# One chunk's square on ScalarE and TensorE instead of VectorE's product, in the edge scoring of a graph attention layer

## The reference

```
h_r   = einsum('nf,hfd->hnd', layernorm(x), W_r)       # 8 heads of 64 features
diff  = h_r[dst] - h_r[src]                            # per edge: 512 numbers
score = s_src + s_dst + sum(diff * a_dif) + sum(|diff| * a_abs) + sum(h_r[src] * h_r[dst] * a_prd)
alpha = leaky_relu(score, 0.2);  att = softmax of alpha over the edges of a source node
out   = sum over edges of att * h_e[dst]
```

## Time and profile before

| what | value |
|---|---|
| median of three runs | 1385.02 us |
| profiled execution | 1381.5 us, its span 1379.7 us |
| TensorE busy | 1239.5 us (90%), weight loads 803.8 us (58%) |
| VectorE busy | 1106.1 us (80%) |
| ScalarE busy | 736.3 us (53%) |
| GpSimd busy | 753.9 us (55%) |
| L794, products, 336 | 229.9 us busy, mean 684 ns |
| L790, subtractions, 204 and 132 | 138.7 and 89.9 us, mean 681 ns |
| L961, sums, 672 records | 91.6 us busy, mean 605 ns |
| L1003 and L1005, ScalarE, 336 each | 196.2 and 273.6 us, mean 584 and 814 ns |
| mean granted TensorE clock | 0.956 of full speed |

### The profile page before, as it was taken

One profiled execution on the slowest core, in us unless ns is written; L12 is line 12 of the kernel. 1 busy time (PEld: TensorE's weight loads), 2 busy tenths in 40 slices (PEclk: granted clock), 3 DMA queues, 4 the chain that ended last, 5 costly groups with the idle time before them and its releaser, 6 DMA issues. The chain is left out here.

```text
span 1379.7 us, 23782 instructions
## 1 busy us (share of the span) xinstructions
PE 1239.5 (90%) x6730; PEld 803.8 (58%) x6805; DVE 1106.1 (80%) x2258; ACT 736.3 (53%) x1237; POOL 753.9 (55%) x858
## 2 busy tenths in 40 slices
PE   6999986989999999999994999999999376999985
PEld 1555553545555555555552888877777244777762
DVE  8989897999999999999997998888888954122216
ACT  5555534888898989989993010000100653555541
POOL 1300016766666666666625777777777502566541
PEclk9999997999999999999996999999999776999998
DMA  9133338988888888888857798888887165343478
GB/s 249 70 122 147 123 124 299 310 290 273 281 300 285 304 294 280 296 285 302 279 167 182 241 318 289 292 296 283 290 268 242 48 228 181 131 134 131 136 256 328
DMA packets 141701, 322.60 MB, mean 234 GB/s; under 512 B 30163, under 2 KB 46279, under 8 KB 141595
## 3 DMA queue, kind: packets, MB, share of 16 engines
q0 software_dynamic: 62816, 212.87, 46.8%
q1 hardware_dynamic: 74524, 103.15, 22.1%
q10 hardware_dynamic: 4256, 5.24, 1.1%
HBM read 255.27 MB, written 65.93 MB: 233 GB/s over the span
## 5 line engine op out<-in xcount | busy, mean ns | idle before, releaser
L1309 PE MATMUL m_ps<-msg,hot 128*128 128x260 f32 x1344 | 304.9, 387 | 14.7 <-SPq L1106 14.7
L1309 PEld LDWEIGHTS m_ps<-msg,hot 128*128 128x128 f32 x1344 | 254.2, 191 | 65.5 <-issue 27.5
L1005 ACT ACTIVATE rows<-rows,raw_a 128x512 f32<-128x512 f32 x336 | 273.6, 814 | 11.2
L1146 POOL DMA_INDIRECT rows<-he_d,target x234 | 237.8, 1016 | 75.1 <-issue 65.5
L929 PE MATMUL gs_ps<-room,hot_t 128*128 x944 | 262.2, 383 | 10.6 <-DVE hot_t L783 3.8
L1227 DVE TENSOR_TENSOR msg<-rows,room 128x512 f32<-128x512 f32 x336 | 213.4, 690 | 40.3 <-DMA rows<-he_d,target 39.1
L794 DVE TENSOR_TENSOR rows<-rows 128x512 f32<-128x512 f32 x336 | 229.9, 684 | 3.1 <-ACT rows L1005 2.8
L1003 ACT ACTIVATE rows<-d_ps 128x512 f32<-128x512 f32 x336 | 196.2, 584 | 62.5 <-PE d_ps L942 61.3
L765 POOL DMA_INDIRECT x_sb<-table_d,target x150 | 148.1, 987 | 80.2 <-PE d_ps L942 48.1
L1163 ACT COPY room<-m_ps 128x520 f32<-128x520 f32 x20 | 11.8, 592 | 296.7 <-PE m_ps L1309 296.7
L929 PEld LDWEIGHTS gs_ps<-room,hot_t 128*128 128x128 bf16 x1008 | 92.0, 98 | 121.3 <-issue 79.1
(11 more groups left out here) (342 smaller groups left out, 1825.7 us busy)
## 6 DMA issues: line engine op xcount, KB each, us to landing
rows<-early_d SPq DMA_DIRECT2D x84, 256.0 KB, 4.3
early_d<-x_sb SPq DMA_DIRECT2D x51, 256.0 KB, 5.4
x_sb<-local_d SPq DMA_DIRECT2D x84, 128.0 KB, 5.1
early_d<-rows SPq DMA_DIRECT2D x33, 256.0 KB, 5.7
table_d<-rows POOLq DMA_DIRECT2D x10, 520.0 KB, 3.3
both_d<-rows POOLq DMA_DIRECT2D x10, 520.0 KB, 4.3
he_d<-he SPq DMA_DIRECT2D x20, 256.0 KB, 2.0
both_d<-he SPq DMA_DIRECT2D x20, 256.0 KB, 2.3
```

The costliest lines, as they stand in the source:

```text
L1005: act.activation(uv[:, j, c, :], ab[:, j, c, :], ACT.Identity, bias=raw[:, 0, c:c + 1], scale=raw[:, 1, c:c + 1]).then_inc(ur, 1)
L1146: pool.indirect_dma_start(g[:, r, t, :, :, :].rearrange("p c h d -> p (c h d)"), None, he_d, bass.IndirectOffsetOnAxis(ap=k["target"][:, q ...
L1309: last = pe.matmul(m_ps[:, bass.ds(slot[t], 1), j, 0:HEADS // 2 * HW].rearrange("p a f -> p (a f)"), hot[:, r, t, :], halves[:, r, t, j, : ...
```

## The change

A group with st below 12 has one squared chunk, c = 3 - st mod 4 (`squared`). For it ScalarE writes diff^2 to one of four buffers (`square`) and |diff| to `ab`, and leaves out w1 * |diff| + w0; VectorE leaves out the product. TensorE sums |diff| of that chunk with w0 as weights in place of ones, in the group's usual sum. Once in four groups, behind the transposes of t = 0, it sums the four squares with w1 as weights (`reduce_squares`). That is 3 rounds a strip, 18 in all. The weights lie in `head_w`, which VectorE fills at the start.

Three of the four square buffers lie in memory that other things used: in the scratch of the strip steps, and in the last strips of `al` and `fw`. The strip steps get their scratch elsewhere, and the third and fourth step of the fifth strip move behind those of the last.

```diff
+SQUARES = STRIPS // CH * CH
+def squared(n):
+    st = n % STRIPS
+    return CH - 1 - st % CH if st < SQUARES else None
...
-        first = home[:, 0:LC]
+        square = (s.sb("square0", [P, LC])[:, :], home[:, 0:LC], al[:, L - LC:L], fw[:, L - LC:L])
...
             def times(n, c):
-                dve.wait_ge(ur, CH * n + c + 1)
+                if c == squared(n):
+                    return
+                dve.wait_ge(ur, rank(n, c))
                 dve.tensor_tensor(uv[:, n % 2, c, :], uv[:, n % 2, c, :], ab[:, n % 2, c, :], ALU.mult).then_inc(vr, 1)
...
+                first = fw[:, hi:hi + LC] if tg < TG - 2 else square[TG - 1 - tg]
                 if step == 2:
                     link(dve.tensor_tensor(first, al[:, lo:hi], lead[:, lo:hi], ALU.add))
...
             link(dve.memset(extra[:, :, :, :, :, :], 0.0))
+            link(dve.memset(k["head_w"][:, :], 0.0))
+            spots = k["head_w"][:, 30:].rearrange("p (i c s) -> p i c s", i=2, c=CH)
+            mark(dve.tensor_copy(spots[0:D, :, :, 0], raw[0:D, :, :]))
+            link(dve.tensor_copy(spots[D:P, :, :, 1], raw[D:P, :, :]))
...
-                        strip_scores((n - 4 - step) // STRIPS - 1, step)
+                        tg = (n - 4 - step) // STRIPS - 1
+                        if tg < TG - 2 or step < 2:
+                            strip_scores(tg, step)
...
             for step in range(4):
                 strip_scores(TG - 1, step)
+            for step in range(2, 4):
+                strip_scores(TG - 2, step)
...
+                    if c == squared(n):
+                        last = pe.matmul(sc_ps[32 * c:32 * (c + 1), :], weight_of(0, c, st), ab[:, n % 2, c, :],
+                                         start=(st == 0), stop=final, tile_position=(0, 32 * c), skip_group_check=True)
...
+            def reduce_squares(n):
+                st = order[n][1]
+                pe.wait_ge(abr, CH * n + squared(n) + 1)
+                for c in range(CH):
+                    of = st - c
+                    last = pe.matmul(sc_ps[32 * c:32 * (c + 1), :], weight_of(1, c, of), square[c],
+                                     start=False, stop=False, tile_position=(0, 32 * c), skip_group_check=True)
+                last.then_inc(squares_red, 1)
...
                     if t == 2 and n >= 2:
                         reduce(n - 2)
+                    if t == 0 and n >= 2 and squared(n - 2) == 0:
+                        reduce_squares(n - 2)
...
+                if c == squared(n):
+                    if rounds(n) >= 1:
+                        act.wait_ge(squares_red, rounds(n))
+                    act.activation(square[c], d_ps[:, c % 2, :], ACT.Square)
                 act.activation(ab[:, j, c, :], d_ps[:, c % 2, :], ACT.Abs).then_inc(abr, 1)
+                if c == squared(n):
+                    return
```

More of the change, by code:

```diff
@@ L723, in score_edges @@
         kept = sem("strip_kept")
+        squares_red = sem("squares_reduced")
+        timed = lambda n: sum(squared(m) != c for m in range(n) for c in range(CH))
+        rank = lambda n, c: timed(n) + sum(squared(n) != d for d in range(c + 1))
+        rounds = lambda n: n // STRIPS * (SQUARES // CH) + n % STRIPS // CH
         early_out = [sem(f"early_out{j}") for j in range(RING)]
@@ L957, in reduce, with weight_of @@
                                   start=False, stop=False, skip_group_check=True)
+                if n == 0:
+                    pe.wait_ge(extras, 1)
+                if squared(n) is not None:
+                    pe.wait_ge(abr, CH * n + CH)
                 for c in range(CH):
                     if n == G - 1 or c == 0:
-                        pe.wait_ge(vr, CH * n + (c + 1 if n == G - 1 else CH))
-                    last = pe.matmul(sc_ps[32 * c:32 * (c + 1), :], heads[:, column], uv[:, n % 2, c, :],
-                                     start=(st == 0), stop=final, tile_position=(0, 32 * c), skip_group_check=True)
-                last.then_inc(red, 1)
+                        pe.wait_ge(vr, rank(n, c if n == G - 1 else CH - 1))
+                    if c == squared(n):
+                        last = pe.matmul(sc_ps[32 * c:32 * (c + 1), :], weight_of(0, c, st), ab[:, n % 2, c, :],
+                                         start=(st == 0), stop=final, tile_position=(0, 32 * c), skip_group_check=True)
+                    else:
+                        last = pe.matmul(sc_ps[32 * c:32 * (c + 1), :], heads[:, column], uv[:, n % 2, c, :],
+                                         start=(st == 0), stop=final, tile_position=(0, 32 * c), skip_group_check=True)
+                last.then_inc(red, 1)
+            def weight_of(i, c, st):
+                lo = 30 + (i * CH + c) * 32 - 2 * st
+                return k["head_w"][:, lo:lo + 32]
+            def reduce_squares(n):
[3 more added lines that the diff above has]
+                    of = st - c
+                    assert squared(n - c) == c
+                    last = pe.matmul(sc_ps[32 * c:32 * (c + 1), :], weight_of(1, c, of), square[c],
+                                     start=False, stop=False, tile_position=(0, 32 * c), skip_group_check=True)
+                last.then_inc(squares_red, 1)
             for n in range(G + 2):
@@ L1940, in kernel_body @@
                 k["not_before"] = flat[:, locals_at + F // 2:locals_at + F // 2 + Q]
+                k["head_w"] = flat[:, locals_at + F // 2 + Q:locals_at + F // 2 + Q + 30 + 2 * CH * 32]
                 k["turns"] = k["pick"].rearrange("p t c s h -> p (t c s h)").bitcast(U16)[0:1, 0:Q]
```

## The result

The changed kernel took 1389.91 us (median of five runs, 1386.90 to 1391.44) against 1385.33 of the kernel before: ratio 1.0042, 95% interval 1.0027 to 1.0056. It is slower, by 4.6 us at the medians; 1390.5 had been predicted.

The account below looks back on a forecast made before the run. TensorE was taken to bound the scoring stage at 5.69 us a plain group. VectorE -15.5, rounds +19.6 and moved steps +1.45 gave +5.5 us: 1390.5 us on the median of 1385.02, range 1384.5 to 1396.

Parts of the forecast that it names:

- TensorE is the pace: Scoring stage: a plain group is TensorE's own 5.69 us; VectorE is late only where something is added to it.
- Rival 1: Scoring stage: hand-overs, not TensorE, set the pace, so the change is faster by about 38 us, 1347 us; chance 0.06.
- the reading by the share of the weight loads: TensorE, plain stretch: weight loads busy only 16.16 of 28.44 us would make it little more than half full.
- A round costs 1.09 us, +19.6 in all: TensorE, scoring: 18 new rounds of four 32-column matmuls, each priced like a group's sum; ends +10.8 to +23.4.
- Rival 2: TensorE, scoring: a round costs only 0.5 to 0.8 us, its weights loading during other matmuls; slightly faster to even; chance 0.12.
- rival 3: Scoring: VectorE gives back 19 us and a round costs 0.99, so the change comes out even, 1385 us; chance 0.14.
- VectorE gives back 15.5 us: Scoring: 72 products fewer recover 11.0 us in the strips' four groups and 4.5 in the first 15 groups.
- The moved steps, +1.45: Stage end: two strip steps of the fifth strip move onto the serial path to the carry exchange, about +1.45 us.
- ScalarE is covered: Scoring: Square and Abs take about 1.2 us, ScalarE's group 5.2, below TensorE's 5.69; no cost, cover 0.5 us a group.
- Rival 4: Scoring: ScalarE becomes late, each 0.1 us beyond 5.7 a group costing 7 us; at 0.1, 1397.5 us; chance 0.06.
- The start is hidden: Before VectorE's first subtraction: a memset of 286 elements and two small copies fit in its 4.48 us idle time; no cost.
- the signs set for being wrong: Changed profile: groups without a round below 5.6 us, a round adding under 0.8 us, or TensorE waiting for ScalarE.

## Why the prediction was right

- *TensorE is the pace.* Right: a plain group stays at 5.7 us while VectorE's busy time in it falls from 27.79 of 28.44 us to 4.74 of 5.70, and taking the rounds out or doubling them moves the stage by 15.9 and 15.4 us. Rival 1, and with it the reading by the share of the weight loads, is excluded: the weight loads are busy 3.24 of 5.70 us (57%), and yet TensorE has no room for a round.
- *A round costs 1.09 us, +19.6 in all.* Right in a plain group (1.10), and for the reason given: the price was read from the same matmuls between the same neighbours, so it holds the 0.24 us of passing to 32 columns and back. The total is 15.9 when the rest stays as it is, since six of the 18 rounds fall beside a scan on VectorE. The prediction knew of that cover and entered it on the other side of the account, in VectorE's gain. Rival 2 is excluded (a round adds 1.10 us in a plain group, not 0.5 to 0.8), and so is rival 3 (VectorE gives back no 19 us). Rival 3's step from sum to next gather is 1.00 us in the earlier trace rows, not 0.99; its sum is 0.5 then, not 0.
- *VectorE gives back 15.5 us.* Counted as the prediction counts, with every round at its full 1.10, the second strip's four groups give 25.24 - 24.08 + 1.10 = 2.26 us and the others' 2.22 (predicted 2.2), and the first 15 groups 94.81 - 93.07 + 3.30 = 5.0 (predicted 4.5): 16.2 in all. As an effect of its own, without the rounds, it is 12.2. So neither term is what its engine does alone; the cover moves some 4 us between them and leaves the sum as it is. Sum of the two terms: +4.1 predicted, +3.7 measured.
- *The moved steps, +1.45.* Measured 1.44, on the serial path.
- *ScalarE is covered.* Right; Square runs 0.58 us, and Square to Abs is 0.48 from start to start (the prediction had about 0.6, so the engine's need was put a little high). Rival 4 is excluded for this kernel; at twice the Squares it begins.
- *The start is hidden.* The first sum came at 232.45 (before 233.18; 232.4 to 233.7 over all runs).

Total 5.5 predicted, 5.1 by the stages, 4.6 by the medians. None of the signs set for being wrong came: groups without a round stay at 5.69 us, a round adds 1.10, and the list of waits after has no TensorE wait for ScalarE. (In the whole stage there is one, 0.70 us behind the last gathers; the kernel before has the same.)

What stays open: why the expert stage is granted 0.99 of the clock in one execution and 0.97 in another. That ratio alone would make 187.74 us into about 191.6 (187.74 x 0.99 / 0.97), most of the way to the 192.03 measured. No run here tests what sets it, nor why the message stage varies.

## What to carry to other kernels

Busy shares did not tell the pace of this stage (98 and 99% of a plain stretch); the constant step between the same instructions, the idle entries and the direction of the waits did. Work taken off an engine that is late in some 33 of 84 groups is worth something only there, so move just that much: 20 products moved made the stage 8 us shorter, 72 moved cost 5 us with the end. When the moved work lands on the engine that sets the pace, price it by the step that the same instructions take in the trace, and put it into the groups in which that engine waits.

## What the runs showed of the hardware

- Behind other 32-column matmuls, a single 32-column fp32 matmul of 512 elements costs TensorE 0.86 us, and four of them on different column strips cost the same 0.86 together.
- The same four matmuls between full-width ones cost 0.24 us more (1.10 against 0.86 us), about 0.09 on entering and 0.13 on leaving.
